# Cross-attention kernel: scores dealt out anew over a step's quarters, even denominators, inverses and a tile's variance in later quarters, and a bank table made from release times

## What is computed

```python
def _L0_xattn_ref(q, k, v):           # 32 query heads, 8 key/value heads, D = 32, softmax over 512 keys
    ...
    scores = jnp.einsum('bkgsd,bktd->bkgst', qh, kh) / scale
    weights = jax.nn.softmax(scores, axis=-1)
    out = jnp.einsum('bkgst,bktd->bkgsd', weights, vh)
...
x = x + _L0_xattn_ref(_layernorm(x, axis=-1), ctx_512, ctx_512)
x = x + _L0_ffn_ref(_layernorm(x, axis=-1), ...)
```

## Time and profile before

| | |
|---|---|
| Runs of the kernel | 1020.99, 1023.92, 1025.22 us (median 1023.92) |
| The profiled execution | 1022.49 us, its span 1020.7 us |
| Granted TensorE clock over the span | 0.995 of full speed |
| Busy share of the span | PE 93%, DVE 88%, POOL 79%, ACT 72% |
| Largest groups on VectorE | row maxima L927: 248 of 2281 ns, 565.8 us |
| Largest groups on ScalarE | exponentials L864: 1024 of 596 ns, 554.7 us |
| Largest groups on GpSimd | front and back sums: 126 of about 4.56 us, 574.9 us |
| Chain that ended last | PE 35%, DVE 31%, issue 25%, ACT 5%, POOL 3% |

### The profile page before, as it was taken

The page is one execution under the profiler, slowest core; times in us unless marked ns, Lnnn a source line. Parts: engine busy times, 40 slices in busy tenths (PEclk is TensorE's granted clock), DMA queues, the critical chain, the costliest instruction groups (busy, mean ns, idle before and its releaser), DMA issues.

```text
span 1020.7 us, 24586 instructions
## 1 busy us (share of the span) xinstructions
PE 947.1 (93%) x9518; PEld 371.1 (36%) x9518; DVE 902.3 (88%) x1106; ACT 730.8 (72%) x1301; POOL 801.6 (79%) x454
## 2 busy tenths in 40 slices
PE   4789999999999999999999999999999999999996
PEld 3223333333333333333333323333222225777773
DVE  6979999999999999999999999998888886888976
ACT  5367788888888888888888877888777777554440
POOL 6259999999999999999999999999999998222110
PEclk9999999999999999999999999999999999999998
DMA  8674776767676767676867685756655744766423
GB/s 246 191 172 109 165 169 155 166 152 169 149 169 154 173 145 176 142 171 148 184 142 179 132 192 129 182 121 153 121 119 138 163 93 147 246 209 233 159 104 164
DMA packets 319875, 164.18 MB, mean 161 GB/s; under 512 B 182216, under 2 KB 307240, under 8 KB 319760
## 3 DMA queue, kind: packets, MB, share of 16 engines
q1 hardware_dynamic: 319456, 161.76, 64.3%
q0 software_dynamic: 304, 0.85, 0.4%
HBM read 107.58 MB, written 54.53 MB: 159 GB/s over the span
## 4 chain that ended last, share of the span: by engine, by line
PE 35%; DVE 31%; issue 25%; ACT 5%; POOL 3%; DMA 1%; SPq 0%; DVEq 0%; POOLq 0%; ACTq 0%
DVE row_max L927 14%; PE psum L590 8%; PE psum L604 6%; PE psum L617 5%; PE psum L735 5%; DVE den_t L939 4%; PE psum L552 4%; ACT probs L864 3%; PE psum L713 3%; DVE o_t L933 3%; DVE probs L1138 2%; PE psum L578 2%; DVE prod_mem L985 2%; PE psum L701 1%; ACT prod_mem L817 1%
## 5 line engine op out<-in xcount | busy, mean ns | idle before, releaser
L864 ACT ACTIVATE probs<-psum 128x512 f32<-128x512 f32 x1024 | 554.7, 596 | 131.0 <-PE psum L590 113.0
L927 DVE TENSOR_REDUCE row_max<-psum 128x4 f32<-128x2048 f32 x248 | 565.8, 2281 | 64.3 <-PE psum L552 64.0
L590 PE MATMUL psum<-q_stack,k_stack 97*32 97x512 f16 x4096 | 334.8, 386 | 9.9 <-issue 3.5
L365 POOL TENSOR_TENSOR sums<-probs 128x2048 f32<-128x2048 f32 x63 | 287.7, 4566 | 17.5 <-ACT probs L864 17.4
L353 POOL TENSOR_TENSOR sums<-probs 128x2048 f32<-128x2048 f32 x63 | 287.2, 4559 | 7.1 <-PE psum L627 5.5
L604 PE MATMUL psum<-probs,v_in 128*32 128x512 f32 x2048 | 268.8, 598 | 1.0
L590 PEld LDWEIGHTS psum<-q_stack,k_stack 97*32 97x32 f16 x4096 | 96.7, 95 | 258.8 <-ACT probs L864 149.2
L552 PE MATMUL psum<-high_mem 32*128 32x512 f16 x992 | 98.0, 384 | 23.7 <-DVE row_max L927 20.1
L325 POOL TENSOR_TENSOR o_t<-o_t,inv 128x512 f32<-128x512 f32 x64 | 67.2, 1049 | 40.7 <-DVE inv L945 38.8
L330 POOL TENSOR_TENSOR o_all<-o_all,o_t 128x512 f32<-128x512 f32 x64 | 81.6, 1274 | 9.2
L604 PEld LDWEIGHTS psum<-probs,v_in 128*32 128x32 f32 x2048 | 59.2, 110 | 60.9 <-issue 16.2
(11 more groups left out here) (119 smaller groups left out, 759.2 us busy)
## 6 DMA issues: line engine op xcount, KB each, us to landing
q_stack<-q_split SPq DMA_DIRECT2D x192, 128.0 KB, 3.4
xa<-in_x_dram SPq DMA_DIRECT2D x32, 512.0 KB, 4.7
o_all<-in_x_dram SPq DMA_DIRECT2D x256, 64.0 KB, 2.4
x_attended<-o_all SPq DMA_DIRECT2D x64, 256.0 KB, 4.1
out_dram<-probs SPq DMA_DIRECT2D x32, 512.0 KB, 2.9
q_split<-prod_mem SPq DMA_DIRECT2D x15, 1024.0 KB, 5.3
xa<-x_attended SPq DMA_DIRECT2D x16, 512.0 KB, 4.5
probs<-x_attended SPq DMA_DIRECT2D x16, 512.0 KB, 4.7
```

The lines of the kernel that those rows point to most:

```text
L365: pool.tensor_tensor(sums[:, 2 * u % SUMS], probs[:, u % 2, 0], probs[:, u % 2, 1], ALU.add).then_inc(front_done, 1)
L590: last = pe.matmul(st_ps[row:row + D, bank_of["score", u, n], :], k_stack[:, u % SLOTS, t * P + row:t * P + row + D], q_stack[:, u % SLOTS ...
L864: act.activation(probs[:, s, keys, g, :], st_ps[:, bank_of["score", u, n], :], ACT.Exp, scale=EXP_SCALE).then_inc(exped, 1)
L927: dve.reduce_max(row_max[:, u % 2, t:G * ST:ST], s_ps[:], AX.X).then_inc(reduced, 1)
```

## The change

The scores of a unit are dealt out 4, 5, 3, 4 (even) and 5, 5, 3, 3 (odd) over the quarters, for 4, 5, 4, 3 and 4, 4, 4, 4; the gathers keep two scores ahead of them, in the last quarter of an odd unit two of three. The bank planner counts time in quarters: each use gets a place in its quarter, a score or turned maximum keeps its bank for 0.4 of a quarter, a part for 0.95, and denominators until the place at which VectorE's program takes them; the parts of a tile are no longer tied to one bank. On VectorE the denominators of an even unit are taken in the second quarter instead of the first (also for the last pair, behind the last sum), its inverse follows in the third quarter, the second half of a tile's moments moves from the second to the third, the variance and the guard from the third quarter of the even unit into the third and fourth of the odd unit that follows. On GpSimd the normalisation of an even unit comes behind the front sum, and so does the inverse root in odd units.

```diff
--- before.py
+++ after.py
@@ -193,35 +193,39 @@
             tile_of = lambda u: (u + AHEAD) // 2 + FIRST
             whole = lambda n: FIRST <= n < TILES
 
-            BEGIN = ((0, 4, 9, 13, NSC), (0, 4, 8, 12, NSC))
-            MIDST = ((2, 6, 11, 15), (2, 6, 10, 14))
+            BEGIN = ((0, 4, 9, 12, NSC), (0, 5, 10, 13, NSC))
+            MIDST = ((2, 6, 11, 14), (2, 7, 12, 15))
             NORM_AT = 13
             DOWN_AT, FOLD_AT = ((-AHEAD, ST - 1), (1 - AHEAD, 0)), (1 - AHEAD, ST - 1)
 
-            filled = [("part", n, i) for n in range(FIRST) for i in range(PIECES)]
+            QUARTERS_KEPT = {"score": 0.4, "max": 0.4, "part": 0.95}
+            DEN_TAKEN_AT = (ST + 2.0, 3.95)
+            filled = [(-LEAD, ("part", n, i)) for n in range(FIRST) for i in range(PIECES)]
             for u in range(-AHEAD, UNITS + 2):
                 for t in range(ST):
                     scores = [("score", u, n) for n in range(BEGIN[u % 2][t], BEGIN[u % 2][t + 1])] if live(u) else []
                     half = MIDST[u % 2][t] - BEGIN[u % 2][t]
+                    now = []
                     if u % 2 == 1 and t < PIECES and whole(tile_of(u)):
-                        filled.append(("part", tile_of(u), t))
-                    filled += scores[:half]
+                        now.append(("part", tile_of(u), t))
+                    now += scores[:half]
                     if t == 2 and live(u + 1):
-                        filled.append(("max", u + 1, 0))
-                    filled += scores[half:]
+                        now.append(("max", u + 1, 0))
+                    now += scores[half:]
                     if t == (ST - 1 if u % 2 == 1 else 2) and live(u - 1):
-                        filled.append(("den", u - 1, 0))
-            KEPT = {"score": 2, "max": 2, "den": (5, 5), "part": 6}
-            bank_of, bank_before, free_at, last_in = {}, {}, [0] * BANKS, [None] * BANKS
-            for i, use in enumerate(filled):
+                        now.append(("den", u - 1, 0))
+                    filled += [(u * ST + t + (i + 1) / (len(now) + 1), use) for i, use in enumerate(now)]
+            bank_of, bank_before, free_at, last_in = {}, {}, [-LEAD] * BANKS, [None] * BANKS
+            for i, (at, use) in enumerate(filled):
                 bank = min(range(BANKS), key=lambda b: free_at[b])
-                if use[0] == "part" and use[1] >= FIRST and use[2] > 0:
-                    bank = bank_of["part", use[1], use[2] - 1]
                 bank_of[use] = bank
                 if last_in[bank] is not None:
                     bank_before[use] = last_in[bank]
-                kept = KEPT["den"][use[1] % 2] if use[0] == "den" else KEPT[use[0]]
-                free_at[bank], last_in[bank] = max(i, free_at[bank]) + kept + 1, use
+                if use[0] == "den":
+                    free_at[bank] = (use[1] + 1) * ST + DEN_TAKEN_AT[use[1] % 2]
+                else:
+                    free_at[bank] = max(at, free_at[bank]) + QUARTERS_KEPT[use[0]]
+                last_in[bank] = use
 
             spare = [i for i in range(BANKS) if i != bank_of["den", UNITS - 1, 0]]
             y_ps = s_ps.rearrange("p (t c) s -> p t (c s)", t=2).rearrange("p t (c m) -> p t c m", m=P)
@@ -355,15 +359,17 @@
                     if u == UNITS - 1:
                         for t in range(ST):
                             row_root(0, 0, t)
-                    if live(u - 2):
+                    if live(u - 2) and u % 2 == 1:
                         normalise(u - 2)
-                    if u % 2 == 1 and whole(tile_of(u) + 1):
-                        inverse_root(tile_of(u) + 1)
                     if 0 <= u < UNITS - 1:
                         wait(pool, exped, NSC * u + NSC // 2)
                         wait(pool, den_done, u - 1)
                         pool.tensor_tensor(sums[:, 2 * u % SUMS], probs[:, u % 2, 0], probs[:, u % 2, 1],
                                            ALU.add).then_inc(front_done, 1)
+                    if live(u - 2) and u % 2 == 0:
+                        normalise(u - 2)
+                    if u % 2 == 1 and whole(tile_of(u) + 1):
+                        inverse_root(tile_of(u) + 1)
 
                 for n in range(ST + 2, TILES):
                     row_root(n // ST, n // ST % GROUPS, n % ST)
@@ -1032,20 +1038,21 @@
                             largest(*maxima_at(u, t))
                         if late and t < PIECES:
                             low_part(n, t)
-                        if t == 0 and live(u - 2) and u % 2 == 0:
-                            take_denominators(u - 2)
                         if u == UNITS and t == 0:
                             sum_last(1)
                         if t == 0 and live(u - 1):
                             take_rows(u - 1)
-                        if t == 1 and live(u - 2):
+                        if t == 1 and live(u - 2) and u % 2 == 0:
+                            take_denominators(u - 2)
+                        if t == (2 if u % 2 == 0 else 1) and live(u - 2):
                             invert(u - 2)
                         if early and t == 0 and u == 0:
                             first_moments(n + 1)
-                        if early and t == 1:
+                        if early and t == 2:
                             last_moments(n + 1)
-                        if early and t == 2:
+                        if late and live(u) and whole(n + 1) and t == 2:
                             variance(n + 1)
+                        if late and live(u) and whole(n + 1) and t == ST - 1:
                             guard(n + 1)
                         if live(u) and u % 2 == 1 and t == ST - 1 and whole(tile_of(u + 1) + 1):
                             first_moments(tile_of(u + 1) + 1)
```

## The result

The changed kernel takes 1074.49 us (median of four runs, 1072.40 to 1076.34) where the kernel before, on the same chip, takes 1024.57. The ratio is 1.049, with a 95% interval of 1.046 to 1.053: slower by about 50 us. The profiled execution took 1074.34 us for a span of 1072.5; it is 51.85 above the profiled execution of before.

The account below looks back on a forecast made before the run. No engine is full; the handing over of row-score banks between VectorE and TensorE bounds each quarter. +1.76 us a pair over 26 pairs (+45.8), +0.5 and +4 for the tail give +50.3, 1074 us; forecast 1056 to 1085, range 1040 to 1092.

Parts of the forecast that it names:

- The loop: Attention quarters (even unit E0 to E3, odd O0 to O3): the later of VectorE and TensorE sets the next; 25.32 us a pair.
- E1: Even unit's second quarter, from its row maximum to the next: two scores' banks for three, forecast 3.40 us, +0.49.
- E2: Even unit's third quarter: loses one score, gains moved VectorE chores; forecast 3.20 us, -0.15.
- The normalisation in E3: Even unit's last quarter: ScalarE's x-tile normalisation delays exponential 13, whose bank score 15 needs; +1.45 us.
- Two banks for three: Even unit's second, odd unit's first and second quarters: third score behind the gather waits for a bank; +0.49, +0.25, +0.77 us.
- The good part: Even unit's third and first, odd unit's last two quarters: moved chores and fewer scores shorten them; together -1.20 us a pair.
- E0: Even unit's first quarter: gives up a VectorE transpose of 0.63; forecast 3.10 us, -0.34.
- The tail: End of the attention: first projection waits for unit 62's denominators, now behind the last sum; +4 us, bounds 0 and 5.1.
- (a): Whole kernel, faster: ScalarE always early, VectorE packed, 23.65 us a pair, 984 to 990 us; chance 0.08.
- (b): Even unit's last quarter: normalisation finds room, two-bank runs still cost; pair 25.92, 1043 us; chance 0.15.
- (c): Whole kernel: stalls replace each other one for one, time within 5 us of now; chance 0.05.
- (d): Whole loop: waits reinforce each other to 27.8 us a pair or more, GpSimd's late sums adding; 1092 us; chance 0.12.

Follow-up runs that it names:

- the best variant: Changed kernel with normalisation ahead of exponential 12, even denominators taken in the even unit's first quarter again, and the old odd deal: 1023.38 us, ratio 1.0007 to the kernel before.

## Why the prediction was right, point by point

**The loop.** The claim that VectorE and TensorE hand the four banks of row scores to and fro, and that the later of the two sets each quarter, carried the whole forecast. The quarters agree with the table to 0.06 us or better in E1, E3, O0, O1 and O3, and the idle times stand where they were foreseen: about 1.4, 0.7 and 0.5 us before O0, O2 and E2 in the text, 1.41, 0.66 and 0.55 in the trace.

**The normalisation in E3.** Forecast +1.45 us for the quarter, measured +1.50, of which 1.21 went when the normalisation was moved by one exponential. Its step from start to the next exponential was put at 1.16; the chain has 1.13 of it. The Trainium skill, "ScalarE: Activation LUTs", What ACT_TABLE_LOAD costs, says that ScalarE operations that run back to back overlap by about 93 ns; the trace agrees, with 1.13 from start to start for an operation of 1.23.

**Two banks for three.** Forecast +0.49, +0.25 and +0.77 in E1, O0 and O1; measured +0.55, +0.25 and +0.78. The early denominators give E1's five scores their third bank back, and E1 is 2.91 again: there the bank is shown to be the cause. The old odd deal (O0 and O1 back at 3.16 and 2.93) takes the fifth score away, and O0 had two banks before as well; five scores with three banks in O0 and O1 were not run, so there the bank's part is worked out and not shown.

**The good part.** Forecast -1.20 over four quarters, measured -0.29, -0.53, -0.29 and -0.24 for E2, O2, O3 and E0, together -1.35. The run with the new deal alone has 1.01 of it, so it is the deal of the scores that shortens these quarters, and VectorE's moved chores add 0.33 and cost 0.55 in E1. E2 and O2 were shorter by 0.14 each than I had put them. I had left in them waits of the kernel before that went with the score that was taken out; that is what the numbers suggest, no run isolates it.

**The tail, the term that was mis-sized.** I put it at 4 us between bounds of 0 and 5.1, and it is 7.3, outside them. The step that failed is the upper bound. It took the delay of the first projection, reckoned from the rows of before, as the most that could be lost. The projection came 8.64 us behind the last sum's start for 2.49 before, 6.15 later and not 5.1, for VectorE's transpose of the result waited for GpSimd longer (4.93 us for 4.00). And TensorE, which had stood still for 5.94 us, came back at half clock: 3.59 us for a projection of 2.09, another 1.50.

**The sum.** 26 pairs by 1.73 are 45.0, six late pairs by 0.16 are 1.0, the tail 7.2: 53.2 against the 51.85 between the two profiled executions. The start of the last sum moved by 44.58 where these terms give 46.0, and VectorE's reductions say how it came to that. First before, then after the change, they mark O1 of unit 1 and O1 of unit 51, 25 pairs apart:

```profile
66.19 2.29 DVE L927 TENSOR_REDUCE row_max<-psum 128x4 f32<-128x2048 f32 x1 [0.36 <-PE psum L552]
...
699.36 2.25 DVE L927 TENSOR_REDUCE row_max<-psum 128x4 f32<-128x2048 f32 x1
```

```profile
65.44 2.29 DVE L933 TENSOR_REDUCE row_max<-psum 128x4 f32<-128x2048 f32 x1 [1.56 <-PE psum L558]
...
94.40 2.29 DVE L933 TENSOR_REDUCE row_max<-psum 128x4 f32<-128x2048 f32 x1 [0.17 <-PE psum L558]
...
743.72 2.29 DVE L933 TENSOR_REDUCE row_max<-psum 128x4 f32<-128x2048 f32 x1 [0.18 <-PE psum L558]
```

Up to there the changed kernel is 0.75 us ahead; the 25 pairs take 45.11 longer; from there to the last sum only 0.22 longer. So 25 pairs carry the 1.73, not the 26 of the forecast, whose first lies in the start-up. And 1.9 of the 45.11 belongs to one pair, the first, of 28.96 us (65.44 to 94.40), with the granted clock at 0.53 between 60 and 70 us; the run with the tail restored, whose loop is the same, has 27.06 there.

The forecast put 46.3 us before the tail and 4 into it; measured are 44.6 and 7.2. The hit to within a microsecond is thus partly luck: the pair was right by itself, one pair too many was counted and one ran slow, and the tail's missing 3 us are about what the rest had too much, together with the offset of 1.4 from the profiled execution to the median, which did not appear in the new runs (0.15).

**The rivals.** The faster one (a) needed exponential 13 within 1.2 us of exponential 12; it came 1.63 after (493.76 to 495.39). The advice that it drew on, to close the gaps of the most occupied engine (the Trainium skill, "Perfetto Trace Analysis", Identifying Performance Opportunities), was not put to the test: no run here closes VectorE's gaps; the change widened them from 1.67 to 2.98, and the best variant leaves 1.62. Rival (b), E3 at 3.12 and a pair of 25.92, failed for the change (4.33 and 27.05), and its numbers came true once the normalisation was moved (3.12 and 25.90). Against (c) the idle places did not only move, they grew; and (d)'s pair of 27.8 was not reached.

## What to carry to other kernels

When several engines are each about 90% busy and none is full, write the steady loop down as one length per step, with the engine that comes last in each, and add the change to that; a chore moved into a gap is worth the gap only if no other engine sets that step. Anything tied to a position in a table (an operation "before number 13") has to be looked at again when the table moves. And a move that is right in the loop is also made in its last round, where its cover is another.

## What the runs showed of the hardware

The price of a long wait on TensorE is more than the wait. In the run of the moves alone, 3.02 us without a matmul brought its granted clock to 0.50 for about 7 us, or in a part of the pairs for 3.5, and made a pair that I had put at 28.1 us one of 30.6 us, or of 29.3 with the shorter stretch. The stalls of up to 1.09 us a quarter in the changed kernel left the clock at 1.00 (400 to 500 us), and the 5.94 us at its end did not. The start-up varies too: the granted clock over the first 60 us was 0.91 in the changed kernel and 1.00 in the variant that differs from it only at the end of the attention, and 0.74 in the run with the later gather.
